# A selective-scan block: VectorE's gate of a chunk moved behind the next scalings but one, and two semaphores made one

## The reference: what is computed

```
dA = exp(dt * A)
h  = h * dA + (dt * xs) outer B          # one step for each token
y  = h . C + D * xs
y  = rmsnorm(y * silu(z)) * gnorm_w
out = y @ out_w.T
```

## Time and profile before

| | |
|---|---|
| time, median of 3 runs | 623.63 us (621.09 to 626.03) |
| the profiled execution | 625.76 us |
| its span | 624.0 us |
| busy: PE / DVE / ACT / POOL | 577.9 / 401.4 / 328.4 / 172.4 us |
| the steady part of the scan (11 chunks) | 119.09 to 190.05 us of the span |
| TensorE's granted clock in it | 1.00 of full speed |

### The profile page before, as it was taken

One profiled execution on the slowest core, in us unless ns is written; L12 is line 12 of the kernel. 1 busy time (PEld: TensorE's weight loads), 2 busy tenths in 40 slices (PEclk: granted clock), 3 DMA queues, 4 the chain that ended last, 5 costly groups with the idle time before them and its releaser, 6 DMA issues.

```text
span 624.0 us, 14105 instructions
## 1 busy us (share of the span) xinstructions
PE 577.9 (93%) x4830; PEld 457.4 (73%) x4831; DVE 401.4 (64%) x997; ACT 328.4 (53%) x711; POOL 172.4 (28%) x190
## 2 busy tenths in 40 slices
PE   7999999898998898987999999998999999999995
PEld 5444457776777565554788888887888999999994
DVE  4986697999999692465456655658766454444441
ACT  3887995877876612356665665564422223332220
POOL 1300006677675401741000000000412332222221
PEclk9999989999999999898999999999999999999998
DMA  7100034564650862007100000043601111111100
GB/s 254 54 1 0 17 102 147 161 194 144 194 163 17 296 258 71 1 1 230 42 18 19 19 11 19 19 154 79 187 17 36 35 33 34 36 33 34 29 17 0
DMA packets 47293, 49.53 MB, mean 79 GB/s; under 512 B 7622, under 2 KB 41642, under 8 KB 47242
## 3 DMA queue, kind: packets, MB, share of 16 engines
q1 hardware_dynamic: 41882, 43.65, 21.9%
q0 software_dynamic: 2208, 5.14, 2.9%
q10 hardware_dynamic: 3152, 0.07, 0.3%
HBM read 39.24 MB, written 5.26 MB: 71 GB/s over the span
## 4 chain that ended last, share of the span: by engine, by line
PE 65%; DVE 18%; issue 7%; ACT 7%; DVEq 1%; POOL 1%; ACTq 0%; POOLq 0%
PE banks L2351 12%; PE banks L2340 12%; PE banks L1808 7%; DVE arena L1257 4%; PE banks L2191 4%; DVE arena L1233 3%; PE banks L2092 3%; PE banks L2216 3%; PE banks L2223 2%; PE banks L2236 2%; PE banks L2103 2%; PE banks L2232 2%; PE banks L1842 2%; DVE ybuf L1474 2%; DVE arena L1243 1%
## 5 line engine op out<-in xcount | busy, mean ns | idle before, releaser
L1053 ACT ACTIVATE prob_b<-banks,gate_w 128x128 f32<-128x128 f32 x92 | 26.3, 368 | 112.0 <-PE banks L2340 111.7
L2351 PE MATMUL banks<-arena,prob_b 128*128 x368 | 83.2, 379 | 0.9 <-issue 0.9
L2340 PE MATMUL banks<-ybuf 128*128 128x128 f32 x560 | 79.3, 276 | 1.9 <-DVE ybuf L1695 1.9
L2351 PEld LDWEIGHTS banks<-arena,prob_b 128*128 128x128 f32 x368 | 68.2, 190 | 9.5 <-issue 1.1
L2340 PEld LDWEIGHTS banks<-ybuf 128*128 128x128 f32 x560 | 71.8, 192 | 3.4 <-DVE ybuf L1695 2.5
L1808 PE MATMUL banks<-featT,ybuf 128*128 128x512 f32 x160 | 70.2, 594 | 1.1 <-ACT featT L692 1.1
L1474 DVE TENSOR_REDUCE ybuf<-banks 128x12 f32<-128x1848 f32 (+1 forms) x32 | 46.1, 1441 | 16.5 <-PE banks L2191 16.5
L1808 PEld LDWEIGHTS banks<-featT,ybuf 128*128 128x128 f32 x160 | 29.8, 190 | 36.6 <-issue 35.0
L1182 DVE SCALAR_TENSOR_TENSOR arena<-arena,conv_w 128x512 f32<-128x512 f32 x72 | 48.9, 743 | 11.3 <-ACT arena L706 11.3
L653 POOL DMA_INDIRECT out<-featT,dts x23 | 23.1, 1005 | 116.2 <-DVE featT L1735 115.9
L624 POOL TENSOR_TENSOR xres<-xres,ybuf 128x256 f32 (+1 forms) x16 | 12.6, 787 | 130.4 <-DVE ybuf L1494 130.4
(11 more groups left out here) (404 smaller groups left out, 1247.3 us busy)
## 6 DMA issues: line engine op xcount, KB each, us to landing
arena<-cum_rows SPq DMA_DIRECT2D x16, 512.0 KB, 4.6
arena<-W1T SPq DMA_DIRECT2D x8, 1024.0 KB, 11.9
arena<-W2T SPq DMA_DIRECT2D x8, 1024.0 KB, 8.8
arena<-arena SPq DMA_DIRECT2D x16, 320.0 KB, 3.2
featT<-ecum_rows SPq DMA_DIRECT2D x30, 128.0 KB, 3.0
xres<-x SPq DMA_DIRECT2D x4, 512.0 KB, 11.1
x_rows<-xres SPq DMA_DIRECT2D x16, 128.0 KB, 2.2
ybuf<-attn_in_wT SPq DMA_DIRECT2D x1, 1288.0 KB, 7.2
```

Source lines behind the costliest of these rows:

```text
L1053: i = act.activation(hidT[:, p, f, :], bank[2 * p + 1][:, (f - 4) * P:(f - 3) * P], ACT.Relu, bias=b1_cols[:, ds(e * NFF + f, 1)])
L2340: m = pe.matmul(bank[2 * p + half][:, f * P:(f + 1) * P], w1_now[k][p][:, (4 * half + f) * P:(4 * half + f + 1) * P], xsT[:, p, k, :], sta ...
L2351: m = pe.matmul(bank[4 + p][:, 0:D], hidT[:, p, f, :], w2_of[:, ds(e * NFF + f, 1), :].rearrange("p a n -> p (a n)"), start=(f == 0), stop ...
```

## The change

VectorE's step t is now: copy of B and the two scalings for t+1, the gate of t-1, the mask for t+1, then sum and state of t and the skip terms of t. The skip terms have a function of their own (`add_skip`), and the gate's multiply of a chunk comes one step later. The mask, now a function (`mask_sides`), stands last of the side work and raises `sides_ready`; `g_ready` is gone, and GpSimd's `make_m` waits for `sides_ready`. In the first two chunks the mask follows both scalings. After the loop the gate of chunk 14 stands ahead of the last sum.

```diff
             def make_m(t, p):
                 pool.wait_ge(S("decay_mat"), t + 1)
-                pool.wait_ge(S("g_ready"), t + 1)
+                pool.wait_ge(S("sides_ready"), t + 1)
...
                 dve.tensor_copy(b_tok[:, p, :], bank[1][:, 0:P])
-                if wait:
-                    dve.wait_ge(S("m_ready"), t - 1)
-                dve.tensor_tensor(gmat[:, p, :], bank[1][:, P:2 * P], tri_le[:, :], ALU.mult).then_inc(S("g_ready"), 1)
...
-                    i = dve.tensor_tensor(dst[:, p, :].rearrange("p (h n) -> p h n", h=H), xv, heads(col[:, ds(t * H, H)], HP), ALU.mult)
-                i.then_inc(S("sides_ready"), 1)
+                    dve.tensor_tensor(dst[:, p, :].rearrange("p (h n) -> p h n", h=H), xv, heads(col[:, ds(t * H, H)], HP), ALU.mult)
+
+            def mask_sides(t, p, wait):
+                if wait:
+                    dve.wait_ge(S("m_ready"), t - 1)
+                dve.tensor_tensor(gmat[:, p, :], bank[1][:, P:2 * P], tri_le[:, :], ALU.mult).then_inc(S("sides_ready"), 1)
...
-            def gate(t, p, wait):
+            def add_skip(t, p):
                 dve.wait_ge(S("intra_added"), t + 1)
...
                 i.then_inc(S("y_ready"), 1)
+
+            def gate(t, p, wait):
...
             chunk_sides(0, 0, False)
+            mask_sides(0, 0, False)
             chunk_sides(1, 1, False)
+            mask_sides(1, 1, False)
             dve.wait_ge(S("conv_done"), NX * NBLK)
             sum_y(0, 0, True)
             add_state(0)
-            gate(0, 0, False)
+            add_skip(0, 0)
 
             def dve_step(t, p, wait=True):
                 chunk_sides(t + 1, 1 - p, True)
+                gate(t - 1, 1 - p, wait)
+                mask_sides(t + 1, 1 - p, True)
                 sum_y(t, p)
                 add_state(t)
-                gate(t, p, wait)
+                add_skip(t, p)
             dve_step(1, 1, False)
-            dve_step(2, 0)
+            dve_step(2, 0, False)
...
+            gate(NT - 2, 0, True)
             sum_y(NT - 1, 1)
+            add_skip(NT - 1, 1)
             gate(NT - 1, 1, True)
```

## The result

The changed kernel takes 636.67 us (median of 4 runs, 636.14 to 637.64) against 623.83 us of the kernel before (4 runs, 621.09 to 626.03): 1.021 times as long, 95% interval 1.0167 to 1.0253. Forecast were 634.9 us and slower. The profiled execution took 637.19 us, its span is 635.5.

The account below looks back on a forecast made before the run. The prediction took VectorE's time for one chunk of the scan as the bound. Thirteen chunks of 7.28 us gave +9.8, start +0.5, end +0.95, together +11.3: 634.9 us against the median, range 621 to 639.

Parts of the forecast that it names:

- VectorE's chunk: VectorE's instructions in one chunk, counted from the copy: gate 1.40, mask 2.01, product 2.21, first skip 4.20 us.
- The moved release: GpSimd's multiply (line 506), released by the later mask, runs 2.44 to 4.80 into the skips; fourth skip at 6.15 us.
- The decay against the fourth skip: GpSimd's decay (line 515), starting at 6.16 to 6.19, goes ahead of VectorE's fourth skip: 7.28 us a chunk.
- the first rival: The fourth skip goes ahead of the decay every time: 6.41 us a chunk, no change, 623.6 us; chance 0.20.
- Start: First two chunks: masks behind both scalings, state's sum 1.2 later, gate gives back 0.7; first full step 0.5 us later.
- End: From the last step's copy to the last gate's end: 0.95 us more than the 10.04 before.
- Sum: 13 chunks of 7.28 us give +9.8 over 84.83; with +0.5 at the start and +0.95 at the end, +11.3 us.
- Faster: Rival: skips keep the port clear of the multiply, TensorE sets 5.76 us a chunk: -8.5, 615 us; chance 0.10.
- the signs: Expected in the new trace: first skip 0.9 to 1.0 us, fourth 1.1 to 1.2, gate 0.69, copies 7.28 apart.
- Rival 4: Slower still than the forecast, by something unseen such as a second operation held in each chunk; chance 0.05.

Follow-up runs that it names:

- a2: Changed kernel with GpSimd's multiply of the decay matrices (line 506) cut to one head of 8, so work is left out: 611.60 us, ratio 0.9795.
- a3: Changed kernel with GpSimd's two additions of squares (lines 520, 522) cut to 8 columns, so work is left out: 617.69 us, ratio 0.9882.
- e1: Changed kernel with nothing left out and a single-column GpSimd product added in front of each decay of the state: 626.16 us, ratio 1.0034.
- b1: Kernel before with only the mask moved behind both scalings, sides and matrix on one semaphore, gate still last: 637.25 us, ratio 1.0226.
- c1: Kernel before with the four skip terms added in PSUM, ahead of the product of line 1243: 616.09 us, ratio 0.9864.
- d1: Kernel before with skip terms added in PSUM and the sum written there too, where the gate reads it: 614.95 us, ratio 0.9847.
- b2: Changed kernel with the mask back ahead of the scalings on its own semaphore, so only the gate is moved: 638.71 us, ratio 1.0212.

## Why the prediction was right, step by step

- *VectorE's chunk.* Gate at 1.39, mask at 1.99, product at 2.19, first skip at 4.18 behind the copy; forecast 1.40, 2.01, 2.21, 4.20. Distances between instructions that don't wait carried over to the new order.
- *The moved release.* Multiply at 2.42 to 4.79 (forecast 2.44 to 4.80). The fourth skip at 6.13 (6.15): the one late chunk of the trace before was the steady state after, as taken. a2 and a3 show both parts of it to be causes.
- *The decay against the fourth skip.* Decay at 6.15 to 6.16 (forecast 6.16 to 6.19, 6.17 taken), held skip, copy at 7.27 (7.28). The step with the thinnest margin; it was argued from one row against the letter of a rule, and e1 shows that 0.06 us the other way would have made it the first rival's 6.4. I gave that rival 0.20. The mechanism was right; that it fell on this side was partly luck, as distances that I knew to a few hundredths decided it.
- *Start.* Forecast 0.5 later, found 1.1 earlier in the profiled execution. TensorE's granted clock was 0.92 of full speed from 84 us to that step before and 1.00 after, and its products ahead of the second chunk's transposes were done 1.6 earlier (97.71 against 96.12); that is -1.6 of clock and 0.5 of change. VectorE's wait for GpSimd ahead of the state's sum grew from 1.08 to 2.27 us, the 1.2 that were forecast. The first two steps together took 14.4 where 14.6 was forecast, though in another way: the first had its decay late and its fourth skip free (6.56), the second its gate held (7.86). TensorE had been idle for 2.42 us ahead of the first, and its mean clock in it was 0.74 of full speed, which the forecast didn't have.
- *End.* 0.85 more (0.95).
- *Sum.* 11.3 forecast, 12.8 between the medians, 11.5 between the spans. Steps gave 9.4 (9.8). What isn't in the forecast is 2.3 us behind the scan at a lower mean clock, and -1.6 ahead of it; both are in single profiled executions. Over the thirteen kernels here the part behind the last gate takes 421.4 to 429.0 us; b1, whose mask is as late, has 421.4, and c1, which is faster than the kernel before, has 429.0. So the 2.3 us don't go with the change; it is luck that they and the -1.6 nearly cancel in the sum.
- *Rivals.* "Faster" would have needed the first skip clear of the multiply; it is held in every chunk. The floor of 5.76 that this rival took for TensorE's was VectorE's own length of a chunk with a free gate, 5.15 + 0.61; d1, with TensorE busy nearly throughout, has 5.67.
- *A slip in the signs.* The first skip was to be 0.9 to 1.0 us long; from the forecast's own 4.20 and 4.80 it comes to 0.75, ending 0.15 behind the multiply, and 0.75 was measured. The total doesn't use it.
- *Rival 4.* "A second operation held in each chunk" didn't come: the gate is 676 ns throughout.

## What to carry to other kernels

When VectorE and GpSimd share a loop, list for each VectorE operation where its two inputs lie, and for each GpSimd operation when it is released; an edit that only reorders instructions can move a long GpSimd operation under a short VectorE one, and the delayed operations then meet further ones of GpSimd: the first skip's wait was 0.4 us, and without it the step was 1.6 us shorter (a2). If an input or the output of such an operation can stay in PSUM (here TensorE's own product, to which the skips could be added), the conflict is gone, and here the operations got no longer by it (1.13 for four skips, 0.70 for the sum). And follow a held operation to whoever waits for it: behind a held gate TensorE stood idle, and its next products ran at a lower clock.

## What the runs showed of the hardware

- Who gets the port when both ask within hundredths of a microsecond. For a fourth skip queued behind the third and a decay of the whole state, over seven kernels: where the decay's start lay from 0.12 us ahead of the skip's to 0.03 behind it, the decay went first in all of them (35 meetings, skip 1.12 to 1.22 us); where it lay 0.07 to 0.28 behind, the skip went first in all of them, at 0.34, and the decay took up to 1.17 where the distance was under 0.2. The third skip ends 0.08 behind the fourth's start, so the change from one to the other lies near the end of the skip ahead. For the gate of the kernel before, which isn't queued behind a running operation, 0.01 decides: a decay 0.016 to 0.020 ahead held the gate (1.57 to 1.58, three times), a decay 0.003 to 0.008 behind let it through at 0.69 and took 1.59 itself (three times). The Trainium skill (SBUF — State Buffer, "Who interferes with whom") has the pair of ports that VectorE and GpSimd share go to whoever issues first. The gate's starts agree; for an instruction that overlaps the one ahead, the starts in the trace are off by 0.03 to 0.07, and here this was worth 10 us of 636.
- The port passes in turn: a waiting skip gets it when the multiply ends even though GpSimd's next operation follows at once (152.32, 0.78 for the 0.72 that it takes beside free skips), and the addition then gets it ahead of the next skip.
- A VectorE operation with one input in SBUF and the other in PSUM, also with its output in PSUM, kept its length beside every GpSimd operation (1.12 to 1.13 for four skips in c1 and d1).
- Where TensorE had stood idle, its granted clock was lower after: behind 3.23 us (b2) it was 0.56 of full speed over the next 3.42 us (1.2 GHz, the lower of its two levels, for most of it), and the projection took 3.42 us for 1.99; behind 2.42 us (changed kernel, first step) it was 0.74 over 6.56 us.
